# Added TensorE products in the seam between the chunks and the experts of a decoder layer

## The reference

```python
x = x + gated_slot_attention(layernorm(x))                       # 4 heads, 64 slots, recurrent over time
x = x + cross_attention(layernorm(x), ctx, ctx, places, mask)    # 16 heads, 64 keys for each batch
x = x + moe(layernorm(x))                                        # 8 experts, top 2, capacity 1280

# moe: tokens in order take places in their experts until these are full
logits = clip(xf @ Wr, -1e4, 1e4);  top_v, top_i = top_k(logits, 2)
pos  = cumsum(onehot(top_i)) - 1;   kept = pos < cap
xe   = rows of xf scattered to (expert, pos)
h    = silu(xe @ W1) * (xe @ W3);   ye = h @ W2
out[token] += weight * kept * ye[expert, pos]
```

## Time and profile before

| | before |
|---|---|
| runs | 1374.69, 1373.56, 1379.21 us; median 1374.69 |
| profiled execution | 1375.09 us, span 1373.1 us |
| granted clock, mean | 0.984 |
| PE busy | 1287.4 us (94% of the span) |
| DVE, ACT, POOL busy | 930.4, 640.0, 420.2 us |
| chain that ended last | PE 81%, DVE 7%, ACT 6%, issue 4% |

### The profile page before, as it was taken

How to read it: one execution, slowest core, us unless ns; L and a number is a source line. 1 busy time by engine, 2 the same in 40 slices (tenths; PEclk the granted TensorE clock), 3 DMA queues, 4 the chain that set the end, 5 groups by cost and what they waited for, 6 DMA issues and landing times.

```text
span 1373.1 us, 33453 instructions
## 1 busy us (share of the span) xinstructions
PE 1287.4 (94%) x11099; PEld 1139.0 (83%) x11099; DVE 930.4 (68%) x2770; ACT 640.0 (47%) x1628; POOL 420.2 (31%) x741
## 2 busy tenths in 40 slices
PE   7899999999999999998599999999999999999996
PEld 5677777777777777776379999999999999999996
DVE  5688888888888888887546565565645656565442
ACT  2555465555555555554335344443434535444331
POOL 4214443443444344333312222222221222222223
PEclk9999999999999999999689999999999999999999
DMA  8600301010101010100052252522524334352222
GB/s 246 181 19 26 126 27 35 26 34 27 34 26 35 27 35 26 34 23 21 28 138 32 32 123 32 124 32 35 128 37 118 37 67 92 36 124 32 32 25 24
DMA packets 152458, 80.18 MB, mean 58 GB/s; under 512 B 106210, under 2 KB 145859, under 8 KB 152290
## 3 DMA queue, kind: packets, MB, share of 16 engines
q1 hardware_dynamic: 137698, 59.11, 17.1%
q0 software_dynamic: 14592, 18.91, 8.2%
HBM read 44.04 MB, written 33.96 MB: 57 GB/s over the span
## 4 chain that ended last, share of the span: by engine, by line
PE 81%; DVE 7%; ACT 6%; issue 4%; POOL 0%; DMA 0%; POOLq 0%; ACTq 0%; DVEq 0%
PE banks L1391 33%; PE banks L1699 32%; PE banks L1500 4%; PE banks L1385 3%; PE banks L1575 2%; PE banks L1586 2%; PE banks L1495 2%; ACT qk_l L807 1%; ACT qk_e L805 1%; PE banks L1571 1%; DVE r_st L939 1%; DVE hk L1064 1%; ACT p_t L727 1%; DVE s_s L1047 1%; ACT one_less L817 1%
## 5 line engine op out<-in xcount | busy, mean ns | idle before, releaser
L912 ACT ACTIVATE h_a<-banks 128x256 f32<-128x256 f32 x320 | 122.3, 382 | 334.3 <-PE banks L1699 321.8
L1322 DVE TENSOR_TENSOR h_f<-banks,h_a 128x256 f32<-128x256 f32 x320 | 135.6, 424 | 138.0 <-ACT h_a L912 116.8
L528 POOL TENSOR_TENSOR idle_g<-half 128x1 f32<-128x1 f32 x144 | 31.5, 219 | 516.3 <-DVE y_s L1341 367.3
L1699 PE MATMUL banks<-xe_t_hi,w_even_hi 128*128 128x256 f32 (+1 forms) x640 | 178.6, 279 | 3.3 <-issue 1.8
L1699 PE MATMUL banks<-xe_t_lo,w_even_hi 128*128 128x256 f32 x640 | 178.2, 278 | 0.0
L1699 PE MATMUL banks<-xe_t_hi,w_even_lo 128*128 128x256 f32 x640 | 178.0, 278 | 0.0
L1699 PE MATMUL banks<-xe_t_hi,w_odd_hi 128*128 128x256 f32 (+1 forms) x640 | 177.7, 278 | 0.0
L1699 PE MATMUL banks<-xe_t_lo,w_odd_hi 128*128 128x256 f32 x640 | 177.4, 277 | 0.0
L1699 PE MATMUL banks<-xe_t_hi,w_odd_lo 128*128 128x256 f32 x640 | 177.3, 277 | 0.0
L901 ACT ACTIVATE h_t_hi<-h_f 128x256 fp32r<-128x256 f32 x320 | 131.7, 412 | 33.9 <-DVE h_f L1322 33.9
L707 POOL DMA_INDIRECT out_dram<-y_s,token x80 | 130.9, 1636 | 26.9 <-issue 20.0
(11 more groups left out here) (246 smaller groups left out, 3393.6 us busy)
## 6 DMA issues: line engine op xcount, KB each, us to landing
raw<-in_w SPq DMA_DIRECT2D x24, 1024.0 KB, 8.7
expert_rows<-empty SPq DMA_DIRECT2D x4, 2580.0 KB, 11.1
x_blocks<-expert_rows SPq DMA_DIRECT2D x312, 32.0 KB
xin<-in_x SPq DMA_DIRECT2D x32, 128.0 KB, 2.2
out_dram<-x SPq DMA_DIRECT2D x32, 128.0 KB, 1.7
out_dram<-y_s,token POOLq DMA_INDIRECT x80, 4.0
mask_i<-in_mask SPq DMA_DIRECT2D x32, 32.0 KB, 1.9
expert_rows<-r_xn,send POOLq DMA_INDIRECT x64, 2.7
```

The costliest lines, as they stand in the source:

```text
L528: return pool.tensor_tensor(idle_g[:, i:i + 1], half[:, 0:1], half[:, 0:1], ALU.add)
L912: act.activation(h_a[:, f % 2, :], bank[2 + f % 4][:, 0:GS], ACT.Silu).then_inc(silu_ok, 1)
L1322: dve.tensor_tensor(h_f[:, f % 2, :], bank[2 + f % 4][:, GS:2 * GS], h_a[:, f % 2, :], ALU.mult)\
L1699: last = pe.matmul(to[:, m * GS:m * GS + cols], lhs, rhs[:, at:at + cols], start=(i == 0), stop=(i == len(pairs) - 1))
```

## The change

Products of the identity with 512 columns of `w_in` are added at eight places of the chunk phase, and the number in `first_columns` goes from 4 to 10. The helper `fill` moves up and takes the tile to write to. The results are overwritten by the product that follows in the same tile. At each place `bank_left` is called for that tile first, then the products are issued, and the step's own waits come behind.

```diff
+            def fill(to, times):
+                for _ in range(times):
+                    pe.matmul(to[:, :], ident[:, :], w_in[:, 0, 0:2 * D], start=True, stop=True)
             def x_columns(n, c, b):
+                if is_last(n, NCH - 1):
+                    bank_left(pe, "x_cols", n)
+                    fill(tile["x_cols"], 2)
                 pe.wait_ge(x_normed, n + 1)
             def e_columns(n, c, b):
+                if is_last(n, NCH - 1):
+                    bank_left(pe, "e_cols0", n)
+                    fill(tile["e_cols0"], 7)
                 pe.wait_ge(ex_ok, n + 1)
             def values(n, c, b):
+                if is_last(n, NCH - 1):
+                    bank_left(pe, "values", n)
+                    fill(tile["values"], 1)
                 pe.wait_ge(et_ok, n + 1)
             def r_columns(n, c, b):
+                if is_last(n, NCH - 1):
+                    bank_left(pe, "r_cols", n)
+                    fill(tile["r_cols"], 6)
                 pe.wait_ge(r_normed, n + 1)
             def r_logits(n, c, b):
+                if is_last(n, NCH - 4):
+                    bank_left(pe, "r_logits", n)
+                    fill(tile["r_logits"], 1)
                 pe.wait_ge(r_cols_ok, n + 1)
+            fill_counts = {NCH - 4: 7, NCH - 2: 2, NCH - 1: 2}
             def counts(n, c, b):
+                if n in fill_counts:
+                    bank_left(pe, "counts", n)
+                    fill(tile["counts"], fill_counts[n])
                 pe.wait_ge(both_ok, n + 1)
                 bank_left(pe, "counts", n)
             def first_columns():
-                fill(4)
+                fill(bank[2], 10)
                 for i in range(4):
                     pe.wait_ge(sent[i], 16 * NCH // 2)
-                fill(3)
+                fill(bank[2], 3)
                 pe.wait_ge(xe_landed, 16)
```

More of the change, by code:

```diff
@@ L1673, in _ @@
             over_chunks(step)
-            def fill(times):
-                for _ in range(times):
-                    pe.matmul(bank[2][:, :], ident[:, :], w_in[:, 0, 0:2 * D], start=True, stop=True)
             def first_columns():
-                fill(4)
+                fill(bank[2], 10)
                 for i in range(4):
                     pe.wait_ge(sent[i], 16 * NCH // 2)
-                fill(3)
+                fill(bank[2], 3)
                 pe.wait_ge(xe_landed, 16)
```

## The result

| | before | changed |
|---|---|---|
| median of five runs, us | 1374.36 (1373.26 to 1379.21) | 1388.33 (1386.4 to 1390.3) |
| ratio to before | | 1.0097, 95% interval 1.0076 to 1.0118 |
| profiled execution, us | 1375.09 | 1388.07 |
| span, us; mean granted clock | 1373.1; 0.984 | 1386.1; 0.992 |
| PE busy, us | 1287.4 | 1311.2 |

A forecast was written before the change was run, and what follows sets the result against it. The seam between chunks and experts was taken as one dependent path whose gains or losses reach the end one for one. Steps 0 + 6.3 + 0.2 + 7.8 - 2.4 + 1.8 = +13.7 gave 1388.4 us, range 1382 to 1393.

The forecast's parts named there:

- Logits 28: One product ahead of logits 28 fits TensorE's 1.19 us wait for r_xnt: 0, bounds 0 to +0.6 us.
- Counts 28: Seven products ahead of counts 28 begin at half clock after the idle stretch; faster work behind returns 1.8: +6.3 us.
- x_xn 31: Two products ahead of the transposes of x_xn 31, 1.7 us in 1.5 idle: +0.2 us.
- ex 31: Seven products ahead of the transposes of ex 31 begin at half clock after about 3.8 us idle: +7.8 us.
- Back from the clock: Work from the transposes of ex 31 on runs at full clock, less small costs of added groups: -2.4 us.
- first_columns: Ten products in place of four ahead of the experts; transposes 11.4 us behind last counts, not 9.55: +1.8 us.
- Rival A: Products run as soon as TensorE is idle and the clock never falls: +1.0 us, 1375.7 us; chance 5%.
- Rival B: Clock stays low longer: both sevens wholly at half, 1396.1 us, or it falls again behind ex 31, 1394.3; chance 9%.
- rival C: One of the two large groups finds its bank early; if ex, +7.4 us in all, 1382.1 us; chance 6%.

The follow-up runs named there:

- the same number early: Changed kernel with both groups of seven writing to bank 2, waiting only for mix of chunk 31 and not for bank 0; ratio 1.0001 to before.
- fitted kernel: Changed kernel with both large groups in bank 2 and groups cut to their idle stretches (5, 5, 1, 1, 1, 5, 7); 1370.95 us, ratio 0.9958 to before.
- second profile of before: The kernel before, unchanged, executed again for another profile; 1379.17 us.
- third profile of before: The kernel before, unchanged, executed a third time for one more profile; 1377.06 us.
- ten products: The kernel before with 10 products in place of 4 in first_columns, nothing else of the change; ratio 1.0012; three profiles of 1376.75, 1378.92 and 1381.13 us.

## Why the prediction was right

Forecast +13.7 us and 1388.4; measured 1388.33, +14.0 between the medians and +13.65 in the timeline of the seam. The steps forecast were the steps found. That the sum meets to 0.1 us is luck all the same, since the seam of one program differs by 1.9 us between executions and the errors of its steps cancel in part. By its steps:

1. Logits 28: 0, as forecast. The product stands in the wait, of which 0.33 us remain.
2. Counts 28: +6.3 forecast, +6.7 measured, with one term too small and one too large. The seven products took 7.8 us, not 8.1, because the clock rose after 3.6 us. The work behind them, put at 2.0 us at full clock, took 2.7 (655.85 to 658.53), so the faster clock gave 1.1 us back and not 1.8. Of the missing 0.7, 0.40 are a wait that I had not named: the transposes of `b_o` share a bank with the state sums and waited for VectorE's `zv` (written from 657.45 to 657.86). Before, `zv` was written by 651.15, a microsecond ahead of these transposes. The other 0.3 are lengths that the sum had too short.
3. x_xn 31: +0.2 forecast, 0 measured: the operand was written at 663.02, and the transposes began at 663.09, right behind the products.
4. ex 31: +7.8 forecast, +7.8 measured. The clock rose 5.0 us after the first product; I had taken 5.1, midway between two rows. This hit is luck as much as method: over all profiles, in the groups of seven and in those in front of the experts that met half clock, it rose 3.0 to 6.1 us after the first product.
5. Back from the clock: -2.4 forecast, -2.5 measured. ScalarE's weight copies were the limit behind the attention products, as forecast: `r_xnt` 30 had its transposes at 686.24 and began only at 686.61, when the copies were through.

```profile
684.72 2.00 ACT L882 ACTIVATE w_even_hi<-raw 128x1024 fp32r<-128x1024 f32 x2
686.61 0.38 ACT L727 ACTIVATE r_xnt<-banks 128x256 f32<-128x256 f32 x1
```

6. first_columns: +1.8 forecast, +1.7 measured (11.29 us behind counts in place of 9.55). The time from the last counts to the gather, which the forecast held fixed, was 7.1 us in place of 6.75 and lies between 6.4 and 7.4 over all profiles; the products hid the difference here.

The two profiled executions differ by 13.0 us: 0.9 us that the changed one was ahead before the seam, 13.65 in it, and 0.3 behind it. Rival A fell with the timeline (no product inside the first idle stretch) and again with the kernel that has the same number early.

The rule of the Trainium skill that long idle gaps between bursts of matmuls return the clock to half (page "TensorE: Matmul & The Clock Gate", section "Why this matters for your kernels") was not wrong: where the gaps are really filled, the clock is worth 1.8 us in one place and 1.1 to 2.2 in the other. It does not cover the falls behind waits of 1.2 us and less that are told in the last section.

Rival B did not come true in the changed kernel, but parts of it did in others. The seven at counts 28 took 9.1 us in the run without products at ex 31, and in the fitted kernel the clock fell again behind ex 31 and the five products at `r_xn` 31 began at half. No run has a group of seven wholly at half, nor one whose bank was free early by itself (rival C).

## What to carry to other kernels

An instruction meant for idle time must stand ahead of every wait that makes the time idle, bank waits too: ask what ends last, the operand or the place to write to, and let filler (products whose results nobody reads) write where nobody else does. Filler costs as much as it runs beyond its wait, at the clock at which it runs, so count its length at full clock and put in no more than fits the wait. A higher mean clock and a busier TensorE are no gain by themselves: here both rose with the time.

## What was not expected of the hardware

- The same idle stretch does not always end in the same clock. Before, 4.36 us idle brought it down within the stretch; in the changed kernel it fell 0.2 us behind 4.26 us of it, and without the products at counts 28 it fell 1.3 us behind the 3.85 us ahead of ex 31. With four products in `first_columns` it fell 0.3 us behind 3.36 us in front of the experts; 1.74 us in the second profile of before did not bring it down.
- In the fitted kernel the clock fell once more from 676.2 to 679.6 us, in a part of the seam whose longest waits are 0.8 and 0.5 us; the mean over its seam is 0.97. Only short waits stood ahead of this fall.

```profile
645.00:696.00 51.00, 44.65 (x229) 23.32 (x228) 26.94 (x96) 12.75 (x27) 18.34 (x41) 0.97 0.12 37
```

- It also fell where there was only one short wait. In the third profile of before, and in the first two with ten products, it went down 1.7 to 2.4 us after logits 28, while TensorE worked without a break behind the 1.19 us that it had waited for `r_xnt`. The products below take 1.14 us at full clock and took 2.08 in the second profile with ten:

```profile
641.11 2.08 PE L1575 MATMUL banks<-k_bd,xq_t 64*128 64x256 f32 x8
```
